# Reading the expert rows back in quarters: each quarter split over two DMA queues by partition halves

## The reference, cut to what matters

```python
x = _layernorm(x + _L0_attn_ref(x, w_qkv, w_out, b_out), axis=-1)       # 16 heads of 8, window of 64 keys
x = _layernorm(x + _L0_ffn_ref(x, gate_w, ..., w3, b3), axis=-1)        # 8 experts, each token goes to its best two
# of an expert:  z = (x w1 + b1) * (x w2 + b2);  s = silu(z wg + bg);  y = s w3 + b3
# of a token:    sum of probs[k] * y of its two experts
```

## Time and profile before

| | us |
|---|---|
| median of three runs | 317.65 |
| lowest and highest run | 317.65, 318.34 |
| the profiled execution, its own time | 318.13 |
| its span, first to last instruction | 316.3 |
| outside the span, in that execution | 1.8 |
| `all_sent` passed, the four reads begin to be issued | at 295.4 of the span |
| first addition on DVE | at 300.2 |
| last activation on ACT ends | at 311.5 |

### The profile page before, as it was taken

One profiled execution on the slowest core, in us unless ns is written; L12 is line 12 of the kernel. 1 busy time (PEld: TensorE's weight loads), 2 busy tenths in 40 slices (PEclk: granted clock), 3 DMA queues, 4 the chain that ended last, 5 costly groups with the idle time before them and its releaser, 6 DMA issues.

```text
span 316.3 us, 7675 instructions
## 1 busy us (share of the span) xinstructions
PE 241.9 (76%) x1791; PEld 177.1 (56%) x1791; DVE 218.1 (69%) x714; ACT 153.3 (48%) x410; POOL 159.2 (50%) x287
## 2 busy tenths in 40 slices
PE   2485798787878788898588775999999999996000
PEld 1154576565667666687355554767677667664000
DVE  5499645778777878786747577687777777674091
ACT  3554636677666677755325542344443443442043
POOL 6654002556566656667763472333455455546151
PEclk9998959999999999999859999899999999999555
DMA  4662625249685968685521021311111111100522
GB/s 130 182 161 68 172 72 135 68 138 272 188 233 168 253 177 233 183 229 181 214 71 37 9 60 36 100 45 52 51 53 37 38 45 53 39 26 7 181 119 99
DMA packets 33988, 36.50 MB, mean 115 GB/s; under 512 B 4972, under 2 KB 30062, under 8 KB 33824
## 3 DMA queue, kind: packets, MB, share of 16 engines
q1 hardware_dynamic: 30864, 29.69, 32.8%
q0 software_dynamic: 2336, 4.37, 4.0%
q10 hardware_dynamic: 752, 2.03, 1.9%
HBM read 25.48 MB, written 11.05 MB: 115 GB/s over the span
## 4 chain that ended last, share of the span: by engine, by line
PE 60%; DVE 11%; ACT 11%; issue 9%; DMA 4%; DVEq 1%; POOL 1%; SPq 1%; ACTq 0%; POOLq 0%
PE bank L1551 10%; PE bank L1523 10%; PE bank L1514 6%; PE bank L1366 5%; PE bank L1370 4%; PE bank L1385 3%; PE bank L1349 3%; PE bank L1395 3%; ACT k_slots L795 3%; PE bank L1546 3%; ACT q_quarters L779 2%; PE bank L1539 2%; PE bank L1347 2%; ACT probs L810 2%; PE bank L1315 2%
## 5 line engine op out<-in xcount | busy, mean ns | idle before, releaser
L713 POOL DMA_INDIRECT expert_out<-probs,tile_x x39 | 40.4, 1035 | 57.7 <-DVE probs L1245 56.2
L810 ACT ACTIVATE probs<-bank 128x512 f32<-128x512 f32 x64 | 35.0, 595 | 39.7 <-PE bank L1370 39.7
L664 POOL DMA_INDIRECT routed<-rows,place x32 | 33.8, 1057 | 21.4 <-issue 16.5
L1523 PE MATMUL bank<-w_gate,x_all 128*128 x156 | 41.2, 388 | 0.4 <-DVE v_aug L1236 0.4
L1551 PE MATMUL bank<-w_up,x_unit 128*128 x78 | 41.4, 613 | 0.0
L949 DVE TENSOR_REDUCE top<-bank 128x4 f32<-128x384 f32 x64 | 33.5, 549 | 8.7 <-PE bank L1349 7.9
L1250 DVE TENSOR_TENSOR w_rows<-bank,b_up 128x512 f32<-128x512 f32 x39 | 26.9, 689 | 17.3 <-PE bank L1551 17.1
L1514 PEld LDWEIGHTS bank<-w_down,xT 128*128 128x128 f32 x156 | 20.8, 193 | 31.9 <-issue 31.9
L959 DVE TENSOR_TENSOR shift<-top,delta_block 64x256 fp32r<-64x256 f32 x64 | 31.0, 485 | 8.5 <-PE bank L1370 6.9
L883 ACT COPY x_unit<-bank 128x128 f32<-128x128 f32 x39 | 10.3, 265 | 53.8 <-PE bank L1531 53.8
L1514 PE MATMUL bank<-w_down,xT 128*128 x156 | 27.4, 299 | 8.2 <-DVE y_in L1231 5.8
(11 more groups left out here) (177 smaller groups left out, 539.6 us busy)
## 6 DMA issues: line engine op xcount, KB each, us to landing
k_stack<-k_scratch SPq DMA_DIRECT2D x28, 160.0 KB, 3.2
q_stack<-q_scratch SPq DMA_DIRECT2D x62, 64.0 KB, 2.3
tile_x<-routed SPq DMA_DIRECT2D x39, 65.0 KB, 1.8
k_scratch<-k_parts SPq DMA_DIRECT2D x7, 320.0 KB, 2.4
q_scratch<-q_parts SPq DMA_DIRECT2D x8, 256.0 KB, 2.4
w_up<-in_L_ffn_w_dram SPq DMA_DIRECT2D x16, 128.0 KB
w_gate<-in_L_ffn_wg_dram SPq DMA_DIRECT2D x8, 256.0 KB
b_up<-in_L_ffn_b_dram SPq DMA_DIRECT2D x2, 1024.0 KB
```

The lines of the kernel that those rows point to most:

```text
L664: eng.indirect_dma_start(routed, bass.IndirectOffsetOnAxis(ap=place[i][:, k:k + 1], axis=0), rows[i][:, k, :], None, bounds_check=SPARE + ...
L713: eng.indirect_dma_start(expert_out, bass.IndirectOffsetOnAxis(ap=tile_x[i][:, P:P + 1].bitcast(I32), axis=0), y[i][:, :], None, bounds_ch ...
L810: eng.activation(probs[t[1] % 2][a][:, 512 * h:512 * h + 512], t_bank[h][:, :], ACT.Exp).then_inc(probs_ready, 1)
L1523: ins = eng.matmul(gate_bank[:, 0:F], zT[m[1] % 2][:, c, :], w_gate[:, bass.ds(e[2], 1), c, :].rearrange("p o n -> p (o n)"), start=(c == ...
```

## The change

`load_two` gets a third argument, a half: it reads the quarter's 4 KB pieces of 64 partitions alone, 256 KB. SP issues the halves of partitions 0 to 63 of the quarters 0, 1, 2, 3, and ACT those of partitions 64 to 127, in the same order. The two DMAs of a quarter raise the same semaphore, and DVE waits for 32 instead of 16. The bytes and the 4 KB pieces are the same; there are eight DMAs for four.

```diff
-        def load_two(eng, q):
-
-            eng.dma_start(y_two[:, 4 * q:4 * q + 4, :, :], two_tokens[:, 4 * q:4 * q + 4, :, :]).then_inc(two_loaded[q], 16)
+        def load_two(eng, q, half):
+
+            r, t = slice(64 * half, 64 * half + 64), slice(4 * q, 4 * q + 4)
+            eng.dma_start(y_two[r, t, :, :], two_tokens[r, t, :, :]).then_inc(two_loaded[q], 16)
+
...
-            for q in (0, 2):
-                load_two(eng, q)
+            for q in range(4):
+                load_two(eng, q, 0)
...
-            for q in (1, 3):
-                load_two(eng, q)
+            for q in range(4):
+                load_two(eng, q, 1)
...
-                eng.wait_ge(two_loaded[q], 16)
+                eng.wait_ge(two_loaded[q], 32)
```

## The result

Over 20 executions each, the changed kernel takes 319.59 us in the median (316.8 to 322.59) and the kernel before 317.78 us. The ratio is 1.0074, with a 95% interval of 1.0045 to 1.0102: slower, by little, but by more than the noise of these executions. The forecast was 317.1, within 316.4 to 318.5.

The account below looks back on a forecast made before the run. Quarter 0's uncovered landing, then DVE's additions and a fixed tail, was taken as the bound. Gaining 0.96 us and losing 0.4 left 0.55 us: span 315.75, profiled execution 317.6, median 317.1, range 316.4 to 318.5.

Parts of the forecast that it names:

- What bounds the kernel: At the kernel's end: quarter 0's uncovered landing, then DVE's four additions at 2.2 us a quarter, then a fixed tail.
- Part 2: Reads into 64 partitions at a time: slower by a factor of 1.2, costing 0.4 us at quarter 0's landing.
- cover of the second quarter: Second quarter's landing, forecast at 301.4, against DVE wanting it at 301.9: 0.5 us to spare.
- Part 3: Added issues, packets and the wait for 32: all hidden, nothing added; later quarters land before DVE wants them.
- Part 1: Quarter 0's landing: needs 64 packets of each queue instead of 128 of one, gaining 0.96 us.
- ACT's late start: ACT's queue at the final reads: starts later than SP's by its nature, not shortened by smaller reads; limits the gain to 0.96 us.
- clean rival: Final reads: factor 1.0 and perhaps an earlier ACT start, gaining 0.96 to 1.2 us; chance 0.28.
- bounds of 1.41 and 1.78: Time factors of the 32-partition reads into `k_stack`, taken as the nearest narrow transfers; at quarter 0 they would cost 0.8 and 1.5 us.
- The rule that was weighed there: Trainium skill on reads into partition halves: two DMAs together gain only 6%, so about 208 GB/s and some 319.3 us.
- The narrow reads: Final reads at 230 GB/s outlast DVE's additions: 0.8 us lost, 318.5, or up to 319.3 at 208 GB/s; chance 0.17.
- No change: Quarter 0 lands at 300.0 to 300.2 as before, through uneven queue turns or a factor of 1.41; 317.5 to 317.7; chance 0.12.
- The signs: Changed profile's end: first addition at 299.6, additions 2.2 us apart, some 330 GB/s, 16.1 us from first addition to end.

Follow-up runs that it names:

- Experiment 4: Changed kernel, but SP reads each quarter's even partitions and ACT the odd ones: median 317.46 us beside 317.25 before (ratio 1.0042); issue to end 20.6 us.
- Experiment 2: Kernel before with six more ways of reading, each twice, ahead of its own reads: 382 GB/s into even and odd partitions, 244 into halves; no whole time given.
- two repetitions: Changed kernel run twice more, unaltered: medians 319.55 us (ratio 1.0008) and 318.0 (0.9884) against before; issue to end 21.8 and 22.0 us.
- first repetition: Changed kernel run again, unaltered: median 319.55 us beside 318.91 before, ratio 1.0008; first addition 5.07 us behind the issue.

## Why the prediction was wrong, point by point

**What bounds the kernel** was right. The end is a transfer without cover, a DVE chain and a fixed tail; every variant's end follows the additions, with 2.2 us to a quarter and no other engine in it.

**The step that failed** is the factor of Part 2, and with it the cover of the second quarter in Part 3, which was worked out from that factor. Experiment 4 keeps all else, the eight requests and the late start of the second queue too: without neighbours the end is 0.4 us shorter than before, with them 0.9 longer. The error in Part 1 alone would have made a smaller gain, but no loss.

**Part 1, 64 packets of each queue (0.96 gained)** was too large: without the neighbours 0.4 was gained at the first landing (4.47 for 4.87 us, experiment 4). It leaned on ACT's late start, which "belongs to the queue and is not shortened by smaller reads". Experiment 2 shows that it goes with the later issue. It also grew: in the changed kernel, from 298 to 299.1, SP has 41 packets and ACT none, more than 2 us behind the issue, where it was 1.6. The start got later, by some 0.5 us, and not sooner as the clean rival thought. The requests of 64 partitions take longer to issue, 0.6 for 0.4 us, and it would fit that the second queue waits behind them, but no run shows that this is the reason. Rows 9, ACT's slower landings elsewhere, were read as a proof of the queue's nature; they also fit one request behind another.

**Part 2, the factor of 1.2** was mis-sized. Measured is 248 GB/s for a share of 102.6%, 242 for a full one, against 409: a factor of 1.7. (The two repetitions move 233 and 239 GB/s, from 300 to 304.) The bounds of 1.41 and 1.78 held it. The choice inside them, half of the smaller excess because the two queues would take turns between the halves, was an argument without a row, and it was wrong: both halves in flight move 230 GB/s where one alone moves 203. What it cost at the first landing, 4.84 against the 4.47 of experiment 4, is the 0.4 us that was forecast, 0.6 in the first repetition; with the factor as far off as it was, that is luck. The loss came one quarter later. The rule that was weighed there was the better guide: the Trainium skill says in "SBUF — State Buffer", under "Can I just issue two DMAs to hit both halves?", that two transfers to two halves gain 6%, and here they gain 13%. The time that the prediction worked out for it has a slip: 0.9 and three times 0.33 are 1.9 us and not 1.7, so 319.5 and not 319.3. That the median of 319.6 lies there is no proof of it, since the end is only 0.9 us longer.

**Part 3** held in its verdict and not in its numbers. The issues hid, though they took 0.6 us each. The cover of the second quarter, 0.5 us, was not there: it landed at 7.9 us behind the issue and not at 6.0. Experiment 4 tells where these 1.9 us come from: there the start of the second queue is as late, and the quarter is complete at 5.7. It is the neighbours and not the late start.

**The rivals.** The narrow reads became the bound in part: a gap of DVE in front of the second addition was the named sign. Its price was 0.8 us, and 0.9 was measured at the end, but that the two agree is luck. It was to be 0.5 at the first landing and 0.1 at each of three more. The first landing came as before, the whole loss arose at the second quarter, which is complete 3.1 us behind the first, and the third and fourth came in time. It had a chance of 0.17, of which 0.05 for so small a loss. Why ACT's half of the second quarter lands 2.0 us behind SP's, when 524 KB at 240 GB/s are 2.2 us in all, is open. "No change" was right about the first addition, for another reason than the two given.

**The signs.** The first addition was to start at 4.3 us behind the issue and came at 4.8; the rate was to be 330 GB/s and was 248, from 302 to 306; the tail of 16.1 us from the first addition became 17.1, 0.9 of it the gap. So the first addition and the end moved by different amounts, which the prediction had named as a sign of being wrong. The other one, an issue of the reads away from 295.4, is worth nothing: that moment varies by itself, from 288.7 to 297.7.

## What to carry to other kernels

Split a read by its free dimension and not by neighbouring partitions: two tokens of all 128 partitions move at 374 GB/s where 64 neighbours of 0 to 63 or 64 to 127 move at 203 to 248. When the first piece of a read is what everything waits for, put all pieces on one queue in the order of need and make the first one small: here the first addition then started 3.0 us behind the issue in place of 4.9, and the end was 0.4 to 1.2 us shorter, though the time of the whole kernel is too coarse to confirm it. The second queue shared the engines and started later. Before a factor between two bounds is chosen for a reason, look for a row for the reason, and without one take the nearest row's value.

## What the runs showed of the hardware

- On one queue, partitions 32 to 95 are read into at 344 GB/s and the even ones at 301 (experiment 2, 317.5 to 319.5, at a share of 88.6%), but 64 to 127 at 216 and 0 to 63 at 203, at full shares. Even and odd ones on two queues move 380. Which rows of the DRAM go where makes no difference to this (382 and 244 GB/s in experiment 2).
- Of two queues that issue at the same moment, one starts later, and both times that ACT issued 0.04 us ahead it was SP. With reads of 128 partitions the later one had 1 packet when the other had 23, or none when it had 21, with reads of 64 none when the other had 37, 41 or 25.
- A read of 64 partitions takes some 0.6 us to issue, whichever 64 they are, and one of 128 partitions 0.4. Why the smaller one takes longer is not known. Its packets start later too: SP's first ones come 1.3 to 1.4 us behind the issue in the changed kernel, and 0.9 to 1.0 in the one before.
